# Building the rotation table in a later stage, spreading the head sums of the expert stage, and taking the layer norm's roots on GpSimd

## The chip, the cores and the metric

The kernel runs on one core of one Trainium2 chip. The metric is the device time of one execution in microseconds; three runs of the kernel before gave 1475.19, 1478.64 and 1481.58 us, so the median is 1478.64 us. The engines are named as in the profile: PE is TensorE's matmul, PEld its weight load, DVE is VectorE, ACT is ScalarE, POOL is GpSimd, and SP is the queue that issues the DMAs.

## The reference

The input is x, 1024 tokens of 512 features in fp32. Eight blocks follow each other, each as `x = layernorm(x + block(x))`, so nothing of one block can start on a tile before the norm of the block before it. What each computes:

- first block: two projections to 128 features, a series of powers of their difference, and a gated feed-forward with 1248 hidden features
- second block, the expert stage: a base product with `W_org`, plus eight low-rank experts whose weights come from a softmax of the mean token. One matrix is built, `w_eff = W_org + delta`, and each token tile is multiplied by it
- third block: attention over a sequence of length 1, so it is a product of x with values and output projection; for each of 8 key/value heads the 4 output matrices of its queries are added, and then merged with the value matrix
- fourth block: a feed-forward with 1792 hidden features whose weights are integers with a zero point and a scale for each group: `(w - z) * s`. This is the quantised feed-forward stage
- fifth block: a stack of four small layers with a long convolution. It needs a table of `p**n` for n from 0 to 1023 for 64 channels and 4 layers, with complex p. Its modulus is applied in a scan; its phase is the rotation table `wave`
- sixth block: a product with two low-rank parts; seventh: causal attention with 32 heads; eighth: a feed-forward with integer weights and one scale for each matrix

## The kernel before, in words

Each stage is a block of five instruction streams that meet at its end. x lies in two forms: `x_tok` (token tiles, 8 of 128x512) and `x_feat` (features on partitions, 128 x 4 x 1024). `x_feat` feeds the matmuls.

**Tail.** The end of every stage, for each token tile t: PE has written the product into one of two banks (`out_ready`); DVE adds it to `x_tok` (L92, or L95 and L97 with a bias), takes the statistics (L98, L99), waits for the standard deviation, takes its reciprocal (L101) and normalises (L102, `normed`). ACT takes the root (L108) and, for the tile before, copies the transposed tile from PSUM to `x_feat` (L115). PE transposes the normalised tile (L134). Each engine works through the tiles in order; DVE waits in place for the root.

**The expert stage** (`lora_then_single_key`). DVE reduces `x_feat` to its mean (L742), PE and DVE turn it into eight coefficients, DVE scales the experts' matrices `up` by them in eight instructions of 64 partitions (L759). Then DVE runs the first part of the rotation table (`Rotation.dve`, L913 to L946: 60 dependent instructions on 128x4 numbers, with two activations of ACT in between), while PE multiplies `down` with the scaled `up` (L694). DVE adds `W_org` (L766), and PE multiplies the eight token tiles by `w_eff` (L610). In the tail loop DVE does, after each tile, the sum of one head group for the next block: `lora_pair` (L774, 128x1024) and `lora_wo_sum` (L777, 128x512). Three buffers hold the heads' matrices, and SP waits for `paired` before it loads a fourth. GpSimd meanwhile doubles the table in ten levels (`Rotation.pool`, L970 to L976): six products on 4·2^level numbers in each level, three in the last, so up to 128x2048. After the tail PE merges the head sums with the value matrix (L707, 64 matmul records), DVE copies the result (L781) and a second tail follows with L610.

**The quantised feed-forward stage** (`swiglu` with `front1`, 14 tiles of hidden features). ACT rounds x to its high part (L379) and DVE subtracts for the low part (L475). For each hidden tile f DVE computes `w - z` (L440), times s (L443, and L445 for the down weights), ACT rounds (L388), DVE takes the low part (L457, `w_lo`). PE does gate and up for both halves of the tokens (48 matmuls, L346), ACT the silu (L395) into a single buffer `gate`, DVE the product with up (L464, `product`). The order on DVE and ACT is written out by hand:

```
split_w_up(0); low part of x; split_w_up(1); [extra_dve]
for each f: multiply(f) for both halves; split_w_up(f + 2)
```

PE may start tile f + 1 only when `product` of the first half of tile f is there, since it writes the same bank. z and s have one buffer each, and SP loads them for the next tile when L445 has used them. After the 14 tiles the hidden features are split into high and low parts (L286 on ACT, L289 on DVE), in two groups g for each token tile, PE multiplies them with the down weights (L363), and the tail runs beside it. PE's transpose of tile t - 1 stands between the two groups of tile t.

**Later stages.** The convolution stage starts when its own weights have landed; its DVE stream waits for the table (`half_ready`). Its tail, the tail of the sixth block and the last feed-forward use the same `Tail`. The causal attention takes its own roots on GpSimd, with an addition (L1507) and a power of -0.5 (L1510).

Of the kernel before, what the change touches and what calls it, by code (L numbers as in the profile page):

```python
# [14 lines left out]
F32 = mybir.dt.float32  # L15
# [19 lines left out]
class Chip:  # L35


    def __init__(self, nc, ctx):
# [13 lines left out]
        self.tails = self.ln_count = 0  # L52
# [10 lines left out]
class Tail:  # L63
# [6 lines left out]
    NAMES = ("out_ready", "out_taken", "ln_step", "var_ready", "std_ready", "normed", "transposed", "feat_ready")  # L70

    def __init__(self, chip, out_bank, tr_bank, last=False):
        self.c, self.out_bank, self.tr_bank, self.last = chip, out_bank, tr_bank, last

        (self.out_ready, self.out_taken, self.ln_step, self.var_ready, self.std_ready, self.normed,
         self.transposed, self.feat_ready) = chip.tail_sems
        self.base = NT * chip.tails
        chip.tails += 1

    def dve(self, dve, t, bias=None):  # L80
# [19 lines left out]
        dve.wait_ge(self.std_ready, self.base + t + 1)  # L100
        step(nc.vector.reciprocal(c.rstd[:, t:t + 1], c.std[:, t:t + 1]))  # L101
# [3 lines left out]
    def act_std(self, act, t):  # L105
# [3 lines left out]
                             bias=c.eps[:, 0:1]).then_inc(self.std_ready, 1)  # L109
# [7 lines left out]
    def act(self, act):  # L117
        for t in range(NT):
            self.act_std(act, t)
            if t and not self.last:  # L120
                self.act_copy(act, t - 1)
# [30 lines left out]
def setup(c):  # L152

    nc = c.nc
    c.eps = c.sb("eps", [P, 1], F32)
    ready, zeroed = c.sem("const_ready"), c.sem("ident_zeroed")
    with nc.Block() as block:

        @block.gpsimd
        def _(pool):  # L160
            nc.gpsimd.memset(c.eps[:, :], EPS)
            nc.gpsimd.memset(c.ident[:, :], 0.0).then_inc(zeroed, 1)
# [57 lines left out]
def swiglu(c, front, down=None, last=None, x_loaded=None, first_loads=None, extra_loads=None,  # L220
           extra_dve=None, extra_pe=None, extra_act=None):
# [15 lines left out]
    with ExitStack() as own:  # L237
# [24 lines left out]
        hidden = sb("hidden", [P, tiles, TOK], F32)  # L262
        g_bank, u_bank = c.bank[0:2], c.bank[2:4]
# [37 lines left out]
        with nc.Block() as block:  # L301

            @block.sync
            def _(sp):
# [18 lines left out]
                if last is not None:  # L323
# [3 lines left out]
                    sp.wait_ge(stored, 16 * NT)  # L327

# [45 lines left out]
            def _(act):  # L374
# [240 lines left out]
def lora_then_single_key(c, a, load_ahead):  # L615
# [16 lines left out]
    with ExitStack() as own:  # L632
# [12 lines left out]
        ones = sb("ones", [P, P])  # L645
# [9 lines left out]
        delta_ready, eff_ready, step = sem("delta"), sem("eff"), sem("step")  # L655

        with nc.Block() as block:

            @block.sync
            def _(sp):  # L660
# [4 lines left out]
                c.rot.load(sp, a)  # L665
                sp.dma_start(w_org[:, :, :], a["L0_org"]).then_inc(org_loaded, 16)
                sp.dma_start(wv[:, :, :], a["L1_wv"]).then_inc(wv_loaded, 16)
                for g in range(KV):
                    if g >= SLOTS:
                        sp.wait_ge(paired, g - SLOTS + 1)  # L670
                    sp.dma_start(wo[:, g % SLOTS, :, :], a["L1_wo"][g]).then_inc(wo_loaded[g % SLOTS], 16)
                load_ahead(sp)

            @block.gpsimd
            def _(pool):
                nc.gpsimd.memset(ones[:, :], 1.0).then_inc(ones_ready, 1)
                c.rot.pool(pool)

            @block.tensor
            def _(pe):  # L680
# [10 lines left out]
                pe.wait_ge(coeff_ready, 1)  # L691
# [40 lines left out]
            def _(dve):  # L732
# [9 lines left out]
                then(nc.vector.tensor_reduce(mean[:, :], c.x_feat[:, :, :], AX.X, ALU.add))  # L742
# [11 lines left out]
                then(nc.vector.tensor_scalar(coeff[:, :], e[:, :], inv[:, 0:1], None, ALU.mult))  # L754
                dve.wait_ge(w_loaded, 32)
                for r in range(RC):
                    for h in range(P // R):
                        rows, expert = slice(h * R, (h + 1) * R), r * (P // R) + h
                        ins = nc.vector.tensor_scalar(up_c[rows, r, :], up[rows, r, :],  # L759
                                                      coeff[rows, expert:expert + 1], None, ALU.mult)  # L760
                ins.then_inc(coeff_ready, 1)
                c.rot.dve(dve)
                dve.wait_ge(org_loaded, 16)
                for i in range(KC):
                    dve.wait_ge(delta_ready, i + 1)
                    nc.vector.tensor_tensor(w_eff[:, i, :], w_org[:, i, :], c.bank[i][:, :], ALU.add)\  # L766
                        .then_inc(eff_ready, 1)
                for t in range(NT):
                    tail.dve(dve, t)

                    dve.wait_ge(wo_loaded[t % SLOTS], 16 * (t // SLOTS + 1))
                    if t:
# [1137 lines left out]
```

## Time and profile before

| | us |
|---|---|
| median of three runs | 1478.64 |
| the profiled execution, whole time | 1483.27 |
| the profiled execution, span from first to last instruction | 1481.6 |
| first block | 0 to 250 |
| expert stage, with the merged attention | 250 to 402 |
| quantised feed-forward stage | 402 to 657 |
| convolution stage | 657 to 842 |
| sixth block | 842 to 890 |
| causal attention | 890 to 1283 |
| last feed-forward | 1283 to 1481 |

The profile is of one execution. Busy time is the time in which an engine had an instruction in work; for matmuls it is modelled, since they are pipelined. PEclk is the mean granted clock of TensorE as a share of full speed: its two levels are 1.2 and 2.4 GHz, so 0.75 of full speed in a window means that half of it ran at the lower level. A timeline row ends in brackets with the idle time before it and what ended it.

### The profile page before, as it was taken

The numbers are of one execution on the slowest core, as the hardware profiler recorded it, in microseconds if no ns is written. First come the engines' busy times: TensorE is split into PE (matmuls) and PEld (weight loads), VectorE is DVE, ScalarE is ACT, GpSimd is POOL, SyncE is SP. The second block draws the span as 40 slices with busy tenths as digits, with TensorE's granted clock in tenths as the row PEclk, the third lists the DMA queues.
The fourth block names the chain that finished last, engine by engine and source line by source line (L and its number), as shares of the span: only waits on it lengthen the run. The fifth ranks groups of instructions, "written<-read, shape, count | busy, mean of one in ns | idle before, by whom it ended". The sixth has DMA issues, their size and how long they took to land. (4 is left out here: it accounts for less than half of the span.)

```text
span 1481.6 us, 14589 instructions
## 1 busy us (share of the span) xinstructions
PE 1285.3 (87%) x5314; PEld 843.9 (57%) x5314; DVE 754.6 (51%) x1301; ACT 426.6 (29%) x709; POOL 142.2 (10%) x208
## 2 busy tenths in 40 slices
PE   7999997869799999973565698989999999699998
PEld 4787664324378887763443243444554553388877
DVE  5223323792655554423556563877777642433254
ACT  2122111100221214210221213136656666312141
POOL 0000000490000000001111004000101114000000
PEclk9999998889989999985566699989999999799999
DMA  7110002450066540004000001000000000021001
GB/s 304 43 42 0 0 0 71 196 195 0 5 222 220 208 153 0 1 15 141 1 0 0 0 0 43 1 1 2 1 2 2 3 3 1 24 83 64 21 19 38
DMA packets 18681, 78.82 MB, mean 53 GB/s; under 512 B 3330, under 2 KB 4226, under 8 KB 16452
## 3 DMA queue, kind: packets, MB, share of 16 engines
q1 hardware_dynamic: 18628, 78.13, 14.6%
q8 instruction: 32, 0.52, 0.1%
q14 instruction: 21, 0.17, 0.0%
HBM read 75.76 MB, written 2.10 MB: 53 GB/s over the span
## 5 line engine op out<-in xcount | busy, mean ns | idle before, releaser
L346 PE MATMUL psum<-L_ffn_x,L_ffn_w_up 128*128 128x512 f32 x1200 | 277.1, 394 | 16.2 <-DVE L_ffn_x L475 16.2
L346 PEld LDWEIGHTS psum<-L_ffn_x,L_ffn_w_up 128*128 128x128 f32 x1200 | 228.4, 191 | 64.5 <-issue 16.6
L1751 DVE TENSOR_REDUCE mqa_top<-psum 128x1 f32<-128x512 f32 (+3 forms) x304 | 186.0, 656 | 59.8 <-PE psum L1577 40.1
L1670 ACT ACTIVATE mqa_prob<-psum 128x512 f32<-128x512 f32 x288 | 160.1, 601 | 87.6 <-PE psum L1595 86.7
L363 PE MATMUL psum<-L_ffn_wd,L_ffn_part_h 128*128 128x512 f32 x600 | 141.6, 397 | 7.0 <-DVE L_ffn_wd L298 7.0
L1595 PE MATMUL psum<-mqa_stack,mqa_keys 100*128 100x512 f32 x288 | 132.7, 475 | 4.7 <-DMA mqa_stack<-mqa_rows 3.4
L363 PEld LDWEIGHTS psum<-L_ffn_wd,L_ffn_part_h 128*128 128x128 f32 x600 | 114.3, 192 | 31.6 <-DVE L_ffn_part_h L289 7.8
L1571 PE MATMUL psum<-mqa_keys,mqa_stack 96*128 96x512 f32 (+3 forms) x384 | 129.3, 384 | 2.3 <-DVE mqa_top L1751 1.0
L346 PE MATMUL psum<-L_attn_x,L_attn_w_up 128*128 128x512 f32 x480 | 111.3, 394 | 3.9 <-DVE L_attn_hidden L464 3.9
L346 PEld LDWEIGHTS psum<-L_attn_x,L_attn_w_up 128*128 128x128 f32 x480 | 91.2, 190 | 23.8 <-issue 4.8
L464 DVE TENSOR_TENSOR L_ffn_hidden<-L_ffn_gate,psum 128x512 f32 (+1 forms) x50 | 34.3, 686 | 138.3 <-PE psum L346 138.3
L1595 PEld LDWEIGHTS psum<-mqa_stack,mqa_keys 100*128 100x128 f32 x288 | 55.3, 196 | 72.0 <-ACT mqa_prob L1670 59.3
L1571 PEld LDWEIGHTS psum<-mqa_keys,mqa_stack 96*128 96x128 f32 x384 | 72.7, 196 | 25.4 <-DVE mqa_top L1751 14.6
L108 ACT ACTIVATE ln_std<-ln_mean_var,eps 128x1 f32<-128x1 f32 x56 | 16.5, 295 | 242.9 <-DVE ln_mean_var L99 242.9
L1608 PE MATMUL psum<-mqa_prob,mqa_v 128*32 128x512 f32 x576 | 77.7, 605 | 0.0
L1108 PE MATMUL psum<-ident,conv_twice 128*128 128x128 f32 x72 | 20.1, 434 | 54.7 <-DVE conv_twice L1220 54.7
L1503 POOL TENSOR_SCALAR_AFFINE_SELECT mqa_prob<-mqa_prob 128x512 f32<-128x512 f32 x64 | 39.8, 640 | 269.6 <-ACT mqa_prob L1670 269.5
L134 PE MATMUL psum<-ident,x_tok 128*128 128x128 f32 x192 | 33.6, 302 | 36.4 <-DVE x_tok L102 35.9
L289 DVE TENSOR_TENSOR L_ffn_part_h<-L_ffn_hidden,L_ffn_part_h 128x896 fp32r<-128x896 f32 (+2 forms) x32 | 31.7, 991 | 58.0 <-ACT L_ffn_part_h L286 58.0
L363 PE MATMUL psum<-L_attn_wd,L_attn_part_h 128*128 128x512 f32 x240 | 61.1, 407 | 0.0
L388 ACT CAST L_ffn_w_up<-L_ffn_stage 128x1024 fp32r<-128x1024 f32 x25 | 26.3, 1050 | 121.0 <-DVE L_ffn_stage L443 81.8
L134 PEld LDWEIGHTS psum<-ident,x_tok 128*128 128x128 f32 x192 | 24.0, 152 | 63.0 <-DVE x_tok L102 57.5
(237 smaller groups left out, 1611.0 us busy)
## 6 DMA issues: line engine op xcount, KB each, us to landing
L_ffn_stage<-in_L_w SPq DMA_DIRECT2D x25, 768.0 KB, 6.6
L_ffn_z_int<-in_L_z SPq DMA_DIRECT2D x14, 768.0 KB, 4.4
L_ffn_s_all<-in_L_s SPq DMA_DIRECT2D x14, 768.0 KB, 6.1
lora_wo<-in_L_wo SPq DMA_DIRECT2D x8, 1024.0 KB, 4.9
L_attn_stage<-in_L_w SPq DMA_DIRECT2D x10, 512.0 KB, 3.6
L_attn_w_down<-in_L_down SPq DMA_DIRECT2D x1, 2560.0 KB, 24.8
x_feat<-in_x_feat SPq DMA_DIRECT2D x2, 1024.0 KB, 7.1
x_tok<-in_x_tok SPq DMA_DIRECT2D x1, 2048.0 KB, 19.2
```

The costliest lines, as they stand in the source:

```text
L134: ins = nc.tensor.transpose(self.tr_bank[t % 2][:, k * P:(k + 1) * P], c.x_tok[:, t, k * P:(k + 1) * P], c.ident[:, :])
L289: nc.vector.tensor_tensor(part_h[:, g, 1, 0:n, :], src, part_h[:, g, 0, 0:n, :].bitcast(F32), ALU.subtract).then_inc(h_lo, 1)
L346: ins = nc.tensor.matmul(bank[half][:, :], w_up[:, slot, w_part, at:at + P], x[:, x_part, k, half * HALF:(half + 1) * HALF], start=k == 0 ...
L363: ins = nc.tensor.matmul(tail.out_bank[t % 2][:, :], part_h[:, g, h_part, f - groups[g].start, :], wd[:, w_part, f, :], start=f == 0 and n ...
L388: nc.scalar.copy(w_up[:, slot, 0, :], stage[:, slot, 0:up_width]).then_inc(w_hi, 1)
L464: nc.vector.tensor_tensor(hidden[:, f, half * HALF:(half + 1) * HALF], gate[:, :], u_bank[half][:, :], ALU.mult).then_inc(product, 1)
L1503: nc.gpsimd.affine_select(out=tile, in_=tile, compare_op=ALU.is_ge, fill=0.0, base=0, pattern=[[0, 4], [1, P]], channel_multiplier=-1).the ...
L1571: ins = nc.tensor.matmul(out[:, at * width:(at + 1) * width], stack[0:SPLIT, head // 2, cols(qt)], keys[0:SPLIT, head % 2, lo:lo + width], ...
L1595: ins = nc.tensor.matmul(score_bank[n % 3], keys[0:SHIFTED, head, cols(kt)], stack[0:SHIFTED, 4 * g:4 * g + 4, cols(qt)], start=True, stop ...
L1608: nc.tensor.matmul(value_bank[row:row + 32, :], v[:, kt, :], prob[:, n % PROBS, :], start=kt == 0, stop=final).then_inc(value_done, 1)
L1670: nc.scalar.activation(prob[:, n % PROBS, :], score_bank[n % 3], ACT.Exp, scale=SCALE)\
L1751: nc.vector.tensor_reduce(top[:, i % 2, lo // HALF, heads[0]:heads[-1] + 1], max_bank[n % 3][:, 0:len(heads) * width] .rearrange("p (h k) ...
```

## The change

- `Rotation` is no longer built in the expert stage. The quantised feed-forward stage gets it through its hooks: the load of its parameters behind the loads for hidden tile 1, `Rotation.dve` on DVE after `split_w_up(1)`, `Rotation.act` on ACT in the same place, `Rotation.pool` on GpSimd once both halves of x are split. Its two big scratch arrays are no longer arrays of their own but views of `x_feat`, which nobody reads from then to the tail. ACT waits for the table's end (`feat_free`) before it splits the hidden features.
- In the expert stage the mean is reduced half by DVE, half by ACT (a copy with an accumulated sum); the scaled `up` is made half by DVE, half by ACT; the head sums are done one before the first `w_eff` tile, one after each of its first two, one after token tiles 2, 4, 6 and 7, and one after the tail. The loads of the heads come earlier in SP's order, those of `W_org` and the value matrix later.
- In every `Tail` the root is no longer ACT's square root and DVE's reciprocal but two GpSimd instructions: the addition of eps, and the power of -0.5. DVE still waits for it in place.

The diff, cut to its core:

```diff
@@ class Tail
-        dve.wait_ge(self.std_ready, self.base + t + 1)
-        step(nc.vector.reciprocal(c.rstd[:, t:t + 1], c.std[:, t:t + 1]))
+        dve.wait_ge(self.rstd_ready, self.base + t + 1)
+        if self.root_on_act:
+            step(nc.vector.reciprocal(c.rstd[:, t:t + 1], c.std[:, t:t + 1]))
         nc.vector.tensor_scalar(row, row, c.mean_var[:, t, 0:1], c.rstd[:, t:t + 1],
                                 ALU.subtract, ALU.mult).then_inc(self.normed, 1)
+    def pool(self, pool):
+        c, nc = self.c, self.c.nc
+        for t in range(NT):
+            pool.wait_ge(self.var_ready, self.base + t + 1)
+            nc.gpsimd.tensor_tensor(c.std[:, t:t + 1], c.mean_var[:, t, 1:2], c.eps[:, 0:1], ALU.add)\
+                .then_inc(self.var_eps, 1)
+            c.var_eps += 1
+            pool.wait_ge(self.var_eps, c.var_eps)
+            nc.gpsimd.tensor_tensor(c.rstd[:, t:t + 1], c.std[:, t:t + 1], c.half_power[:, :], ALU.pow)\
+                .then_inc(self.rstd_ready, 1)
@@ def swiglu
+            @block.gpsimd
+            def _(pool):
+                if extra_pool is not None:
+                    pool.wait_ge(x_lo, base["x_lo"] + 2)
+                    extra_pool(pool)
+                tail.pool(pool)
@@ act, before the split of the hidden features
+                if feat_free is not None:
+                    act.wait_ge(feat_free, 1)
@@ act, in the token loop
-                    tail.act_std(act, t)
@@ def lora_then_single_key, sync
-                c.rot.load(sp, a)
-                sp.dma_start(w_org[:, :, :], a["L0_org"]).then_inc(org_loaded, 16)
-                sp.dma_start(wv[:, :, :], a["L1_wv"]).then_inc(wv_loaded, 16)
                 for g in range(KV):
                     if g >= SLOTS:
                         sp.wait_ge(paired, g - SLOTS + 1)
                     sp.dma_start(wo[:, g % SLOTS, :, :], a["L1_wo"][g]).then_inc(wo_loaded[g % SLOTS], 16)
+                    if g == 1:
+                        sp.dma_start(w_org[:, :, :], a["L0_org"]).then_inc(org_loaded, 16)
+                    if g == SLOTS:
+                        sp.dma_start(wv[:, :, :], a["L1_wv"]).then_inc(wv_loaded, 16)
@@ gpsimd
-                c.rot.pool(pool)
+                tail.pool(pool)
+                tail_values.pool(pool)
@@ scalar
+                for k in range(2, KC):
+                    nc.scalar.activation(wide_sum[:, k - 2, :], c.x_feat[:, k, :], ACT.Copy,
+                                         accum_out=mean[:, k:k + 1]).then_inc(mean_by_act, 1)
...
-                c.rot.act(act)
+                act.wait_ge(w_loaded, 32)
+                act.wait_ge(step, COEFF_STEP)
+                for r in range(RC):
+                    ins = nc.scalar.activation(up_c[0:R, r, :], up[0:R, r, :], ACT.Copy,
+                                               scale=coeff[0:R, 2 * r:2 * r + 1])
+                ins.then_inc(coeff_ready, 1)
@@ vector
-                then(nc.vector.tensor_reduce(mean[:, :], c.x_feat[:, :, :], AX.X, ALU.add))
+                then(nc.vector.tensor_reduce(mean[:, 0:2], c.x_feat[:, 0:2, :], AX.X, ALU.add))
+                dve.wait_ge(mean_by_act, 2)
...
-                c.rot.dve(dve)
+                add_heads(0)
                 dve.wait_ge(org_loaded, 16)
                 for i in range(KC):
                     dve.wait_ge(delta_ready, i + 1)
                     nc.vector.tensor_tensor(w_eff[:, i, :], w_org[:, i, :], c.bank[i][:, :], ALU.add)\
                         .then_inc(eff_ready, 1)
+                    if i in (0, 1):
+                        add_heads(i + 1)
                 for t in range(NT):
                     tail.dve(dve, t)
+                    if t in (2, 4, 6, 7):
+                        add_heads(3 + (2, 4, 6, 7).index(t))
+                add_heads(7)
@@ class Rotation, scratch
-        self.other = c.sb("rot_other", [P, C_DEPTH, TOK // 2], F32, own)
-        self.tmp = c.sb("rot_tmp", [P, C_DEPTH, TOK // 2], F32, own)
+        self.other, self.tmp = (c.x_feat[:, 2 * i:2 * i + 2, :].rearrange("p a (b n) -> p (a b) n", b=2)
+                                for i in range(2))
@@ def build
-            lora_then_single_key(c, a, front1.load_first)
-        swiglu(c, front1)
+        lora_then_single_key(c, a, front1.load_first)
+        swiglu(c, front1, extra_scratch=c.rot.scratch, extra_loads=lambda sp: c.rot.load(sp, a),
+               extra_dve=c.rot.dve, extra_act=c.rot.act, extra_pool=c.rot.pool, feat_free=c.rot.half_ready)
```

`add_heads(g)` is the pair of DVE instructions of L774 and L777 with their waits.

## Rows read from the trace of the kernel before

**Rows 1.** Busy time by window: PE, PEld, DVE, ACT, POOL; then PEclk, DMA share, GB/s.

```profile
250.00:402.00 152.00, 119.50 (x298) 55.25 (x298) 95.47 (x181) 18.29 (x39) 53.30 (x68) 0.87 0.29 113
402.00:655.00 253.00, 238.14 (x1036) 194.47 (x1036) 132.31 (x156) 64.49 (x91) 0.00 (x0) 0.97 0.33 118
```

**Rows 2.** Timeline, expert stage up to its first products: start, duration, instruction, idle before.

```profile
250.18 4.42 DVE L742 TENSOR_REDUCE lora_mean<-x_feat 128x4 f32<-128x4096 f32 x1 [1.91 <-PEq L301]
...
259.47 3.96 DVE L759 TENSOR_SCALAR lora_up_c<-lora_up,lora_coeff 64x512 f32<-64x512 f32 x8 [0.16 <-DMA lora_down<-in_L_lora_down]
263.58 16.77 PE L694 MATMUL psum<-lora_up_c,lora_down 128*128 128x512 f32 x32 [5.62 <-DVE lora_up_c L759]
...
281.13 7.13 PE L610 MATMUL psum<-lora_w_eff,x_feat 128*128 128x512 f32 x16 [0.78 <-DVE lora_w_eff L766]
```

**Rows 3.** Timeline, expert stage, DVE and POOL together, and PE's merge.

```profile
325.96 4.58 POOL L972 TENSOR_TENSOR wave<-wave,rot_tmp 128x2048 f32<-128x2048 f32 x1
326.08 5.54 DVE L774 TENSOR_TENSOR lora_pair<-lora_wo 128x1024 f32<-128x1024 f32 x1
334.91 1.22 DVE L774 TENSOR_TENSOR lora_pair<-lora_wo 128x1024 f32<-128x1024 f32 x1
335.96 9.49 PE L707 MATMUL psum<-lora_wo_sum,lora_wv 128*128 128x512 f32 x16
345.72 20.77 PE L707 MATMUL psum<-lora_wo_sum,lora_wv 128*128 128x512 f32 x48
```

**Rows 4.** Timeline, second tail of that stage, one of its tiles on DVE.

```profile
382.20 0.69 DVE L92 TENSOR_TENSOR x_tok<-x_tok,psum 128x512 f32<-128x512 f32 x1 [1.13 <-PE psum L610]
```

**Rows 5.** Timeline, first and last of the 60 DVE instructions of the rotation.

```profile
263.46 0.16 DVE L913 SCALAR_TENSOR_TENSOR rot_small<-rot_par 128x4 f32<-128x4 f32 x1
...
275.21 0.17 DVE L946 COPY rot_small<-rot_small 128x4 f32<-128x4 f32 x1
```

**Rows 6.** Timeline, DVE in the quantised feed-forward stage.

```profile
412.51 1.76 DVE L440 TENSOR_TENSOR L_ffn_stage<-L_ffn_stage,L_ffn_z_int 128x1536 f32<-128x1536 int32 x1 [0.44 <-DMA L_ffn_s_all<-in_L_s]
...
416.64 1.23 DVE L457 TENSOR_TENSOR L_ffn_w_up<-L_ffn_stage,L_ffn_w_up 128x1024 fp32r<-128x1024 f32 x1 [0.51 <-ACT L_ffn_w_up L388]
...
424.07 0.69 DVE L464 TENSOR_TENSOR L_ffn_hidden<-L_ffn_gate,psum 128x512 f32<-128x512 f32 x1 [4.75 <-PE psum L346]
```

**Rows 7.** Busy time by window of PE alone, from its first matmul of that stage: PE, PEclk, DMA.

```profile
409.90:424.00 14.10, 13.99 (x49) 0.78 0.70 265
424.00:435.00 11.00, 11.00 (x50) 1.00 0.52 174
```

**Rows 8.** POOL's groups by form: busy us, mean ns, idle before.

```profile
L971 POOL TENSOR_TENSOR wave<-wave,rot_turn 128x2048 f32<-128x2048 f32 x1 | 3.9, 3929 | 0.1
L970 POOL TENSOR_TENSOR rot_tmp<-rot_other,rot_turn 128x1024 f32<-128x1024 f32 x1 | 1.9, 1892 | 0.1
```

**Rows 9.** Timeline, DVE's wait for the root: by ACT, then by POOL in attention.

```profile
399.69 0.16 DVE L101 RECIPROCAL ln_rstd<-ln_std 128x1 f32<-128x1 f32 x1 [0.36 <-ACT ln_std L108]
399.88 0.55 DVE L102 TENSOR_SCALAR x_tok<-x_tok,ln_mean_var,ln_rstd 128x512 f32<-128x512 f32 x1
...
1280.84 0.55 DVE L1792 TENSOR_SCALAR x_tok<-x_tok,ln_mean_var,ln_rstd 128x512 f32<-128x512 f32 x1 [0.93 <-POOL ln_rstd L1510]
```

**Rows 10.** Timeline, tail of the quantised feed-forward stage: one turn of its loop.

```profile
600.97 0.94 ACT L286 CAST L_ffn_part_h<-L_ffn_hidden 128x896 fp32r<-128x896 f32 x1 [4.06 <-PE psum L363]
...
605.14 0.55 DVE L102 TENSOR_SCALAR x_tok<-x_tok,ln_mean_var,ln_rstd 128x512 f32<-128x512 f32 x1
...
605.75 0.42 PEld L134 LDWEIGHTS psum<-ident,x_tok 128*128 128x128 f32 x4 [0.47 <-DVE x_tok L102]
```

**Rows 11.** Timeline, the additions of two tiles in the convolution's tail.

```profile
829.20 0.68 DVE L92 TENSOR_TENSOR x_tok<-x_tok,psum 128x512 f32<-128x512 f32 x1
...
831.85 0.68 DVE L92 TENSOR_TENSOR x_tok<-x_tok,psum 128x512 f32<-128x512 f32 x1
```

**Rows 12.** Timeline, the addition of one tile in the sixth block's tail.

```profile
869.11 0.69 DVE L95 TENSOR_TENSOR x_tok<-x_tok,psum 128x512 f32<-128x512 f32 x1 [0.41 <-PE psum L610]
```

**Rows 13.** The page, part 6, DMA issues of the expert stage: KB each, us from issue to landing.

```profile
lora_wo<-in_L_wo SPq DMA_DIRECT2D x8, 1024.0 KB, 4.9
```

More of the change, by code:

```diff
@@ L51, in __init__ @@
         self.ffn_base["loaded"] = [0, 0]
-        self.tails = self.ln_count = 0
+        self.tails = self.ln_count = self.var_eps = 0
         psum = ctx.enter_context(nc.psum_tensor("psum", [P, 8, 512], F32))
@@ L63, with __init__ @@
 class Tail:
-    NAMES = ("out_ready", "out_taken", "ln_step", "var_ready", "std_ready", "normed", "transposed", "feat_ready")
-    def __init__(self, chip, out_bank, tr_bank, last=False):
+    NAMES = ("out_ready", "out_taken", "ln_step", "var_ready", "var_eps", "rstd_ready", "normed", "transposed",
+             "feat_ready")
+    def __init__(self, chip, out_bank, tr_bank, last=False, root_on_act=False):
         self.c, self.out_bank, self.tr_bank, self.last = chip, out_bank, tr_bank, last
-        (self.out_ready, self.out_taken, self.ln_step, self.var_ready, self.std_ready, self.normed,
+        self.root_on_act = root_on_act
+        (self.out_ready, self.out_taken, self.ln_step, self.var_ready, self.var_eps, self.rstd_ready, self.normed,
          self.transposed, self.feat_ready) = chip.tail_sems
@@ L220, in swiglu @@
 def swiglu(c, front, down=None, last=None, x_loaded=None, first_loads=None, extra_loads=None,
-           extra_dve=None, extra_pe=None, extra_act=None):
+           extra_dve=None, extra_pe=None, extra_act=None, extra_pool=None, extra_scratch=None,
+           feat_free=None):
     nc = c.nc
@@ L262, in swiglu @@
         hidden = sb("hidden", [P, tiles, TOK], F32)
+        if extra_scratch is not None:
+            extra_scratch(own)
         g_bank, u_bank = c.bank[0:2], c.bank[2:4]
@@ L754, in _, with add_heads @@
                 then(nc.vector.tensor_scalar(coeff[:, :], e[:, :], inv[:, 0:1], None, ALU.mult))
+                assert count == COEFF_STEP, count
                 dve.wait_ge(w_loaded, 32)
                 for r in range(RC):
[L757 to L760, printed above, removed]
+                    ins = nc.vector.tensor_scalar(up_c[R:P, r, :], up[R:P, r, :], coeff[R:P, 2 * r + 1:2 * r + 2],
+                                                  None, ALU.mult)
                 ins.then_inc(coeff_ready, 1)
-                c.rot.dve(dve)
+                def add_heads(g):
+                    dve.wait_ge(wo_loaded[g % SLOTS], 16 * (g // SLOTS + 1))
+                    if g:
+                        dve.wait_ge(summed, g)
+                    nc.vector.tensor_tensor(pair[:, :, :], wo[:, g % SLOTS, 0:2, :], wo[:, g % SLOTS, 2:4, :],
+                                            ALU.add).then_inc(paired, 1)
+                    dve.wait_ge(paired, g + 1)
+                    nc.vector.tensor_tensor(wo_sum[:, g, :], pair[:, 0, :], pair[:, 1, :], ALU.add)\
+                        .then_inc(summed, 1)
+                add_heads(0)
                 dve.wait_ge(org_loaded, 16)
@@ L767, in _ @@
                         .then_inc(eff_ready, 1)
+                    if i in (0, 1):
+                        add_heads(i + 1)
                 for t in range(NT):
                     tail.dve(dve, t)
-                    dve.wait_ge(wo_loaded[t % SLOTS], 16 * (t // SLOTS + 1))
-                    if t:
-                        dve.wait_ge(summed, t)
-                    nc.vector.tensor_tensor(pair[:, :, :], wo[:, t % SLOTS, 0:2, :], wo[:, t % SLOTS, 2:4, :],
-                                            ALU.add).then_inc(paired, 1)
-                    dve.wait_ge(paired, t + 1)
-                    nc.vector.tensor_tensor(wo_sum[:, t, :], pair[:, 0, :], pair[:, 1, :], ALU.add)\
-                        .then_inc(summed, 1)
+                    if t in (2, 4, 6, 7):
+                        add_heads(3 + (2, 4, 6, 7).index(t))
+                add_heads(7)
                 for i in range(KC):
@@ L820, in two_loras, with _ @@
         with nc.Block() as block:
+            @block.gpsimd
+            def _(pool):
+                tail.pool(pool)
             @block.tensor
@@ L1089, in _ @@
                 root(2 * C_DEPTH)
+                tail.pool(pool)
             @block.tensor
```

21 lines of the change are left out of this document (10 added, 11 removed).

## The prediction

> **What bounds the kernel now.** I read the windows by stage first. PE is busy 119.5 of the expert stage's 152 us, and 238.1 of 253 us in the quantised feed-forward stage, whose clock is 0.97; the reader is to see that only the first has much to give, and that DVE (95 us) and POOL (53 us) work beside each other there [rows 1]. The timeline of the expert stage says why PE waits. An instruction of L774 takes 1.22 us alone, and 5.54 us while POOL's L972 runs (325.96 to 330.54); it ends 1.1 us after POOL does [rows 3]. So the two do not share, one waits for the whole instruction of the other, and between two of POOL's a DVE instruction gets its turn. L92, which reads PSUM, keeps its 0.68 us throughout. From the first product's end at about 284.9 (281.13 plus half of 7.13 [rows 2]) to the start of the merge at 335.96 [rows 3] eight tiles take 51 us, 6.4 each, while in the second tail a tile is 3.87: 2.74 of DVE and 1.13 of waiting for PE, which is the bound there [rows 4].
>
> In the quantised stage PE runs without a gap, 48 matmuls in 10.9 us, once started [rows 7]. DVE is busy 7.4 of each 10.9: it is off the path by 3.5 us a tile. The table goes there.
>
> **The change, part by part.** Times are those of the profiled execution (1483.27, span 1481.6).
>
> *The front of the expert stage: -1.6.* Half the mean on ACT saves half of 4.42, but DVE already waits 0.16 for `lora_down` before L759 [rows 2]; that load keeps its place in SP's order, so only 0.16 is saved there. Of the eight L759 instructions (3.96) DVE keeps four, 2.0; ACT's four are not in the trace. ACT's L286 takes 0.94 for 896 columns [rows 10], so 0.6 for 512, and I take 2.4; bounds 2.0 to 4.0. -1.6 at PE's start; the 16.77 of L694 only moves. L913 to L946 took DVE from 263.46 to 275.4 [rows 5], wholly beside L694, whose last tile decides (280.4): removing it saves nothing. The first three head sums (1.22 + 0.69 each) go into that same cover. `W_org` now lands behind two head loads of 1 MB; a head load takes 4.9 from issue to landing [rows 13], in a queue of several at once, so an estimate of 10 us for both puts it before 268, and up to about 275 nothing waits, since only the last of the four additions decides.
>
> *The tails of the expert stage: -23.2.* Without POOL a DVE tile is 2.65 (L92 to L92, [rows 11]), plus 0.37 for the new root (below), so 3.0. Head sums of 1.9 after tiles 2, 4 and 6 make two tiles 7.9 against PE's 7.7; two product banks cover the difference. So 3.9 a tile. First output at 284.9 - 1.6 = 283.3; seven more are out at 310.7, the transposes of tile 6 make it 311.1. Before 335.96, less 1.6: 24.8 - 1.6 = 23.2. The heads' loads (SP waits for `paired`) are each asked 8 us or more ahead. The sums behind tile 7 end at 318.6, PE wants the last at about 335.
>
> *The merge: -2.6.* The first 16 records took 9.49, where 48 took 20.77, so 6.9 for 16 [rows 3]: PE had waited for L102 before and came at a low clock. That wait is gone. The second tail stays PE-bound (3.0 against 3.87). Expert stage: **-27.4**; bounds -20 (tiles at 4.5, clock not gained) to -30.
>
> *`Rotation.dve` in the quantised stage: +9.4.* DVE ends `split_w_up(1)` at 417.87 and has 60 instructions before it, 11.9 us: until 429.7, then L464 until 430.4. Before, PE ended tile 0 at 424.0 and went on at once, since that product had been made early [rows 6]. It now waits 6.4 us. ACT's roots and three table loads end by 423 and hide under this. After 8.9 us of idling PE's first tile took 14.0 instead of 10.9 with a granted clock of 0.78 [rows 7]: +3.1; before L694 it had idled 5.6 and lost 2.9. I take +3.0 for 6.4. Bounds 6.4 to 9.5.
>
> *`Rotation.pool` beside DVE: +12.5.* Each hidden tile has four DVE instructions with two SBUF inputs (L440 1.76, L443 1.2, L445 0.7, L457 1.23 [rows 6]), like L774. Each can wait for one whole instruction of POOL, and then POOL takes the port before the next. Levels 0 to 6 are POOL instructions of 0.2 to 0.6 us: up to 2.4 a tile, inside the 3.5. They last until about 456. Level 7, six of some 1.05: 4.2 in the tile, covered by 3.5 and the early finish before it. Level 8, six of 1.89, and level 9, three of about 3.65 alone (3.9 with waits) [rows 8]: one tile meets four of 1.9, 7.6 us, less 3.5 and about 0.3 of lag: 3.8 late. The next meets two of 1.9 and two of 3.65, 11.1, less 3.5, less 2.0 by which the low clock stretches PE's tile, less 0.9 for the one already under way: 4.7 late. The ninth-level instruction that is left falls in a tile with cover. Two waits of 4 us: two low-clock starts. The merge above lost 2.6 after 3 us; I take 2.0 each. 8.5 + 4.0 = 12.5. Bounds: 0, and, if all fifteen of levels 7 to 9 (28.6 us) are met, less 3.5 in four tiles, 14.6 plus three starts of 3.0, 23.6. Table complete at about 500, `feat_free` asked at 566: free.
>
> L440 reads int32, and no row shows such a one beside POOL. The Trainium skill (SBUF — State Buffer, "SBUF: two separate sides") calls the pair of ports between the two engines "an exclusive lock, not a bandwidth split", taken by any DVE instruction with two SBUF inputs. By that rule L440 counts and the sum stays; if it did not, each tile would meet three: 5.7 less 3.5 less 0.3 is 1.9, the next 9.2 less 3.5 less 0.9 is 4.8, and with one low-clock start the sum would have 8 to 9 in place of 12.5. The trace agrees for fp32 (5.54 against 1.22).
>
> *The roots: +7.8.* DVE waits 0.36 for ACT and then spends 0.16 + 0.04 on L101: 0.56. Where POOL makes the root, it waits 0.93 [rows 9]: **+0.37** a tile. Bounds: 0.2, 0.6. Where does it show? In the quantised stage's tail a turn is a closed chain: output, ACT L286 at 600.97, DVE L289, L92 to L102 (ends 605.69), PEld L134 at 605.75 having waited 0.47 for it [rows 10], then PE's second group, next output. Seven turns and the end: 8 x 0.37 = 3.0. The convolution's tail is DVE's alone, 2.65 a tile [rows 11]: 8 x 0.37 = 3.0. In the sixth block DVE waits only 0.41 a tile [rows 12]: 0.37 nearly fills that, and I take 0.7 with its end. First block, second tail of the expert stage and the last feed-forward: only the last tile, 1.1. ACT's five table loads for the root all lay in idle time and give nothing.
>
> **Sum:** -27.4 + 9.4 + 12.5 + 7.8 = **+2.3**, so 1485.6 for an execution like the profiled one. That one was 4.6 over the median of 1478.64; on the median it is **1481.0**.
>
> **The rivals.**
> - *The lock does not reach PE.* For: DVE has 3.5 us spare a tile, two buffers of `w_up`, and many of POOL's instructions fall in DVE's free time. Against: four instructions a tile, and POOL lost no turn in [rows 3]. Then 12.5 falls to 0 to 3: 1481.0 - 11 = 1470 (faster).
> - *The lock and the clock take more* (slower). POOL's three long instructions all meet one hidden tile: 3 x 3.65 + 1.9 = 12.9, less 3.5: 9.4; the tile before 7.9 - 3.5 = 4.4; starts 3 + 2. That is 18.8 in place of 12.5, and 1487.3. It decides once the first level-9 instruction is asked within the four of one tile, which a shift of 1 to 2 us in POOL's start brings about. With five percent longer POOL instructions too, 1491.
> - *The expert stage gives less.* DVE stays the bound of its tails at 4.5 a tile (8 x 0.6 = 5) because the loads of heads wait on `paired`, and the merge keeps its low clock (2.6): 1488.6. Against: all these loads have slack above.
> - *Nothing of it does what it says*, the table still waits in the expert stage: no, the queues show its instructions gone.
>
> **How the numbers follow.** 0.5% is 7.4 us, about what can be told from no change. Forecast, 0.45: 1481, own range 1474 to 1486. Lock not felt, 0.25: 1467 to 1474. Lock and clock, 0.18: 1486 to 1494. Less from the expert stage, 0.12: 1484 to 1493. The unknown sizes (12.5 between 0 and 23.6, 27.4 between 20 and 30) would allow 1466 to 1500; their far ends together are unlikely: range **1466 to 1494**. Faster than 1471.2: 0.22. Slower than 1486.0: 0.30. Between: 0.48.
>
> **What would show it.** Expert stage about 125 us instead of 152, L774 at 1.22 throughout, L707 in one run of 28. In the quantised stage a PE gap of 6 us before its second hidden tile; L440 to L457 of 2 to 5 us around the fifth and sixth, gaps of 4 there, none later. DVE idle 0.93 before each L102, the turn of that stage's tail 10.6 instead of 10.25, the convolution's tail 3.0 a tile. Wrong if L440 keeps 1.76 beside a long POOL instruction, if PE's gap before tile 1 is absent, or if the expert tails stay over 4.5.

## The result, and the profile after

The changed kernel takes **1481.99 us** (median of 20 runs, 1478.29 to 1486.42); the kernel before, beside it, 1478.39 (20 runs). The ratio is 1.0027, 95% interval [1.0017, 1.0036]: 4 us slower, inside the 0.5% that the prediction called the same. Forecast: 1481.0, as +2.3 on 1478.64. The profiled execution took 1483.97 (span 1482.2, clock 0.906), against 1483.27 (1481.6) before.

Busy time by window of the kernel after (columns as in [rows 1]). The first window starts as there and ends 27 us earlier; the second is as long as there:

```profile
250.00:375.00 125.00, 109.83 (x298) 51.92 (x298) 59.17 (x101) 15.25 (x26) 12.02 (x33) 0.92 0.34 137
375.38:628.00 252.62, 223.28 (x942) 181.38 (x943) 150.29 (x193) 59.60 (x81) 66.81 (x77) 0.93 0.33 119
```

The expert stage has lost its POOL work (53.30 to 12.02) and 27 us. The quantised stage has it now (0 to 66.81), PE is busy 223.28 instead of 238.14 of as many microseconds, and its clock fell from 0.97 to 0.93: a window of that length no longer holds the whole stage.

The path of PE through the expert stage (timeline: start, duration, instruction, idle before), to be laid beside [rows 2, 3]:

```profile
262.70 16.39 PE L724 MATMUL psum<-lora_up_c,lora_down 128*128 128x512 f32 x32 [6.64 <-ACT lora_up_c L763]
...
279.87 7.13 PE L637 MATMUL psum<-lora_w_eff,x_feat 128*128 128x512 f32 x16 [0.78 <-DVE lora_w_eff L816]
...
311.22 7.03 PE L737 MATMUL psum<-lora_wo_sum,lora_wv 128*128 128x512 f32 x16
```

The product with `w_eff` (L637) starts 1.3 earlier than before, the merge (L737) 24.7 earlier, and its first 16 records take 7.03, not 9.49. On DVE, in the same stretch, a tile with a head sum and one without:

```profile
293.94 1.22 DVE L806 TENSOR_TENSOR lora_pair<-lora_wo 128x1024 f32<-128x1024 f32 x1
...
295.80 0.68 DVE L94 TENSOR_TENSOR x_tok<-x_tok,psum 128x512 f32<-128x512 f32 x1
...
298.36 0.55 DVE L105 TENSOR_SCALAR x_tok<-x_tok,ln_mean_var,ln_rstd 128x512 f32<-128x512 f32 x1 [0.93 <-POOL ln_rstd L122]
298.82 0.68 DVE L94 TENSOR_TENSOR x_tok<-x_tok,psum 128x512 f32<-128x512 f32 x1
...
303.70 0.68 DVE L94 TENSOR_TENSOR x_tok<-x_tok,psum 128x512 f32<-128x512 f32 x1
```

From addition to addition (L94) it is 3.02 us without a head sum and 4.88 with one. The sum's first instruction (L806) takes its 1.22, and DVE waits 0.93 for the root.

PE in the quantised stage, every run of matmuls that began after an idle time until the end of the up phase:

```profile
383.65 12.73 PE L372 MATMUL psum<-L_ffn_x,L_ffn_w_up 128*128 128x512 f32 x48 [8.87 <-DVE L_ffn_x L502]
404.17 45.35 PE L372 MATMUL psum<-L_ffn_x,L_ffn_w_up 128*128 128x512 f32 x192 [7.79 <-DVE L_ffn_hidden L491]
452.79 13.96 PE L372 MATMUL psum<-L_ffn_x,L_ffn_w_up 128*128 128x512 f32 x48 [3.27 <-DVE L_ffn_hidden L491]
470.97 89.57 PE L372 MATMUL psum<-L_ffn_x,L_ffn_w_up 128*128 128x512 f32 x384 [4.22 <-DVE L_ffn_hidden L491]
```

The 7.79 stands behind the 60 instructions of `Rotation.dve`, which begin and end so on DVE:

```profile
391.50 0.15 DVE L963 SCALAR_TENSOR_TENSOR rot_small<-rot_par 128x4 f32<-128x4 f32 x1
...
403.26 0.17 DVE L996 COPY rot_small<-rot_small 128x4 f32<-128x4 f32 x1
403.34 0.69 DVE L491 TENSOR_TENSOR L_ffn_hidden<-L_ffn_gate,psum 128x512 f32<-128x512 f32 x1
```

The lock is the name used here for what [rows 3] showed: of a DVE and a POOL instruction that meet, one waits for the other. It stands behind the 3.27 and the 4.22. DVE before the first of them:

```profile
441.76 1.90 DVE L467 TENSOR_TENSOR L_ffn_stage<-L_ffn_stage,L_ffn_z_int 128x1536 f32<-128x1536 int32 x1 [2.21 <-DMA L_ffn_s_all<-in_L_s]
...
443.69 3.31 DVE L470 TENSOR_TENSOR L_ffn_stage<-L_ffn_stage,L_ffn_s_all 128x1024 f32<-128x1024 f32 x1
...
446.93 2.38 DVE L472 TENSOR_TENSOR L_ffn_w_down<-L_ffn_stage,L_ffn_s_all 128x512 f32 x1
...
449.23 2.91 DVE L484 TENSOR_TENSOR L_ffn_w_up<-L_ffn_stage,L_ffn_w_up 128x1024 fp32r<-128x1024 f32 x1
```

DVE and POOL before the second:

```profile
454.44 3.60 POOL L1020 TENSOR_TENSOR x_feat<-x_feat,rot_turn 128x2048 f32<-128x2048 f32 x1
456.21 3.45 DVE L467 TENSOR_TENSOR L_ffn_stage<-L_ffn_stage,L_ffn_z_int 128x1536 f32<-128x1536 int32 x1 [1.95 <-DMA L_ffn_s_all<-in_L_s]
458.12 5.00 POOL L1021 TENSOR_TENSOR wave<-wave,rot_turn 128x2048 f32<-128x2048 f32 x1
459.69 4.51 DVE L470 TENSOR_TENSOR L_ffn_stage<-L_ffn_stage,L_ffn_s_all 128x1024 f32<-128x1024 f32 x1
463.20 5.44 POOL L1022 TENSOR_TENSOR wave<-wave,x_feat 128x2048 f32<-128x2048 f32 x1
464.12 5.07 DVE L472 TENSOR_TENSOR L_ffn_w_down<-L_ffn_stage,L_ffn_s_all 128x512 f32 x1
469.11 1.21 DVE L484 TENSOR_TENSOR L_ffn_w_up<-L_ffn_stage,L_ffn_w_up 128x1024 fp32r<-128x1024 f32 x1
```

Read the ends: L470 ends 1.08 after POOL's L1021 (464.20, 463.12), L472 0.55 after L1022. Each ended within its own time (1.23, 0.68) of the other's end. POOL's instructions waited in turn: L1021 took 5.00 and stood for 1.54 of it beside L467 (which ended at 459.66), L1022 5.44, of which 1.00 beside L470.

Not all of DVE's lateness is waiting for POOL. In both tiles L467 first waited for the load of the scales, 2.21 and 1.95 us. z and s have one buffer, so that load is asked only when L472 of the tile before has ended (449.31; asked at 449.46 and 449.89, there at 456.2). A late L472 makes the next tile's load late as well.

### The profile page after: what moved, and what is told of

Same layout as the page of the kernel before. It is cut to its first block and busy times, and to the rows that moved or that the text cites. A ratio compares the mean times of both kernels' runs of the same rounds, so it can differ in the third digit from the quotient of the medians.

```text
span 1482.2 us, 14587 instructions
## 1 busy us (share of the span) xinstructions
PE 1286.5 (87%) x5314; PEld 844.7 (57%) x5314; DVE 740.3 (50%) x1241; ACT 406.7 (27%) x652; POOL 193.5 (13%) x320
## 5 line engine op out<-in xcount | busy, mean ns | idle before, releaser
L372 PE MATMUL psum<-L_ffn_x,L_ffn_w_up 128*128 128x512 f32 x1200 | 283.3, 399 | 31.5 <-DVE L_ffn_x L502 16.2
L372 PEld LDWEIGHTS psum<-L_ffn_x,L_ffn_w_up 128*128 128x128 f32 x1200 | 232.1, 194 | 82.5 <-issue 25.0
L118 POOL TENSOR_TENSOR ln_std<-ln_mean_var,eps 128x1 f32<-128x1 f32 x56 | 10.6, 190 | 779.5 <-DVE ln_mean_var L101 779.5
L129 ACT COPY x_feat<-psum 128x512 f32<-128x512 f32 x48 | 28.0, 584 | 200.5 <-PE psum L149 200.5
L421 ACT ACTIVATE L_ffn_gate<-psum 128x512 f32<-128x512 f32 x50 | 29.8, 596 | 107.6 <-PE psum L372 87.5
```

Source lines behind the costliest of these rows:

```text
L129: nc.scalar.copy(c.x_feat[:, :, t * P:(t + 1) * P], src).then_inc(self.feat_ready, 1)
L372: ins = nc.tensor.matmul(bank[half][:, :], w_up[:, slot, w_part, at:at + P], x[:, x_part, k, half * HALF:(half + 1) * HALF], start=k == 0 ...
L421: nc.scalar.activation(gate[:, :], g_bank[half][:, :], ACT.Silu).then_inc(gated, 1)
```

## The experiments

The ratio is always to the kernel before, on the same chip; "against the changed kernel" is the difference of two such ratios times 1478 us, good to about 3 us.

**Roots on ScalarE again.** ACT makes the root and DVE its reciprocal, in every tail but attention's, the quantised one's included; POOL's part of `Tail` goes.

```
-    def __init__(self, chip, out_bank, tr_bank, last=False, root_on_act=False):
+    def __init__(self, chip, out_bank, tr_bank, last=False, root_on_act=True):
...
                     if t + 1 < NT:
                         split_h(act, t + 1, 1, 0)
+                    if tail.root_on_act:
+                        tail.act_std(act, t)
```

> The changed kernel (1482.0) with one part undone: all tails take the root by ACT's square root and DVE's reciprocal again. Theory: the root on GpSimd costs 0.37 us wherever DVE's chain is closed; against the trace of before, the changed kernel lost 3.1 in the tail of the quantised stage, 2.6 in the convolution's, 1.3 in the sixth block's and 0.4 at each of three other ends. So 1482.0 - 8 = 1474 (1473 to 1476), ratio to before 0.997. Rival: DVE is not the bound of most tails, the wait is hidden, and the trace's shifts are chance: 1480 to 1482.

Measured: 1471.34 us, ratio 0.9958 [0.9943, 0.9974], 10 us less than the changed kernel. In the convolution's tail (timeline, DVE; first the kernel after, then this one):

```profile
819.64 0.68 DVE L94 TENSOR_TENSOR x_tok<-x_tok,psum 128x512 f32<-128x512 f32 x1
...
822.20 0.55 DVE L105 TENSOR_SCALAR x_tok<-x_tok,ln_mean_var,ln_rstd 128x512 f32<-128x512 f32 x1 [0.94 <-POOL ln_rstd L122]
822.66 0.68 DVE L94 TENSOR_TENSOR x_tok<-x_tok,psum 128x512 f32<-128x512 f32 x1
```

```profile
819.26 0.16 DVE L104 RECIPROCAL ln_rstd<-ln_std 128x1 f32<-128x1 f32 x1 [0.36 <-ACT ln_std L111]
819.46 0.55 DVE L105 TENSOR_SCALAR x_tok<-x_tok,ln_mean_var,ln_rstd 128x512 f32<-128x512 f32 x1
```

0.94 of waiting against 0.36 + 0.16 + 0.04: the 0.37 a tile of the prediction. Stretch by stretch, the changed kernel's trace is longer than this one by 0.4 in the first block, 0.7 and 0.8 in the two tails of the expert stage, 3.3 in the quantised tail, 2.2 in the convolution's, 1.1 in the sixth block's and 0.4 at the end: 8.8 us. That the roots cost about what they were said to is shown; 10 with an error of 3 holds the 7.8 forecast.

**The table in pieces.** Each multiplication of `Rotation.pool` is cut into pieces of 64 columns (256 elements a partition); nothing else.

```
+PIECE = 64
...
-            src, dst = slice(0, n), slice(n, 2 * n)
-            then(mul(tmp[:, :, src], other[:, :, src], sin, ALU.mult))
+            for at in range(0, n, PIECE):
+                src, dst = slice(at, min(n, at + PIECE)), slice(n + at, n + min(n, at + PIECE))
+                then(mul(tmp[:, :, src], other[:, :, src], sin, ALU.mult))
...
```

> The changed kernel (1482.0) with the GpSimd instructions of the three largest doubling levels cut into pieces of 256 numbers (60 pieces of about 0.6 us instead of 15 of 1.0 to 3.6); the same work and a little more GpSimd time. Theory (a DVE instruction waits for one whole GpSimd instruction): each of four DVE instructions a hidden tile waits at most 0.7, 2.8 a tile, under DVE's 3.5 us of spare time, so both gaps of PE around tiles 5 and 6 (3.3 and 4.2) and the two low-clock starts (5.6) go: 1482.0 - 13 = 1469 (1467 to 1472). Rival (the two engines share a bandwidth, so what counts is the total GpSimd work in the stage): 1482 to 1486, the gaps smaller but more.

Measured: 1468.89 us, ratio 0.9957 [0.9940, 0.9974]. PE's second run of matmuls now has no end before the phase has:

```profile
403.91 143.19 PE L372 MATMUL psum<-L_ffn_x,L_ffn_w_up 128*128 128x512 f32 x624 [7.89 <-DVE L_ffn_hidden L491]
```

In the changed kernel the same 624 matmuls lie between 404.17 and 560.54, 156.4 us: 13.2 more, of which 7.5 are gaps and 5.7 low clock. DVE's groups around levels 8 and 9 (busy us, mean ns), of the kernel after (440 to 500 us) and of this one (420 to 500):

```profile
L470 DVE TENSOR_TENSOR L_ffn_stage<-L_ffn_stage,L_ffn_s_all 128x1024 f32<-128x1024 f32 x5 | 11.5, 2298 | 0.2
...
L472 DVE TENSOR_TENSOR L_ffn_w_down<-L_ffn_stage,L_ffn_s_all 128x512 f32 x5 | 9.5, 1900 | 0.0
```

```profile
L470 DVE TENSOR_TENSOR L_ffn_stage<-L_ffn_stage,L_ffn_s_all 128x1024 f32<-128x1024 f32 x8 | 11.8, 1481 | 0.3
...
L472 DVE TENSOR_TENSOR L_ffn_w_down<-L_ffn_stage,L_ffn_s_all 128x512 f32 x7 | 7.6, 1093 | 0.0
```

POOL has as much to compute and is busy longer (69.95 us of the window 375 to 480 instead of 63.09, and 21.36 instead of 5.19 of the next 170). It is not POOL's time in all that cost PE anything, but the length of a single instruction of POOL against the time that DVE has to spare in a tile.

**The table without its long levels.** Levels 7 to 9 are left out, so that the scan starts from an incomplete table (the array is filled with ones early on).

```
-        for level in range(self.LEVELS):
+        for level in range(7):
```

> The changed kernel (1482.0) without the three largest doubling levels on GpSimd (the rest of the rotation table is only filled with ones, in the expert stage, so the result is another). Theory: PE's gaps around hidden tiles 5 and 6 and their low clock come from these levels alone: 1482.0 - 13 = 1469, as with the pieces. Rival: the gaps come from the z and s loads that wait for L472 (DVE waited 2.2, 2.0 and 3.6 us for them): 1476 to 1480, and the gaps stay in part.

Measured: 1469.79 us, ratio 0.9948 [0.9930, 0.9967].

```profile
402.26 144.60 PE L372 MATMUL psum<-L_ffn_x,L_ffn_w_up 128*128 128x512 f32 x624 [8.07 <-DVE L_ffn_hidden L491]
```

That gap is the last one of the up phase here too, though levels 0 to 6 still meet DVE. Leaving the long levels out gives what cutting them gives, within the error. The whole of that term came from them. The recorded rival, that the loads of z and s make the gaps, fails as far as the loads alone go: here L467 waits at most 0.57 for them, and in the run with pieces of 64 it waits up to 2.84 while PE runs without a gap. Their waits add to a tile that the lock has made late; no run gave z and s a second buffer, so the size of that part is not tested.

**Pieces of 256 columns.** As above with `PIECE = 256`: level 9's three instructions are halved, to the length of level 8's; level 8 is untouched.

> Changed kernel with pieces of 256 columns (1024 elements a partition), so that only the three instructions of level 9 are cut, in two; level 8 keeps its length. Theory (the price goes by the longest POOL instruction that the four DVE instructions of one tile meet, and PE has 3.5 us of cover): level 9's waits halve and their gap of 4.2 us goes with its low clock, level 8's gap of 3.3 us with its low clock stays: -6, 1476, ratio 0.9985. Rival (any shortening is enough, or it is POOL's total that counts): as pieces of 64, ratio 0.996, or nothing at all, 1.003.

Measured: 1478.24 us, ratio 1.0005 [0.9992, 1.0017], 3 less than the changed kernel.

```profile
454.20 12.56 PE L372 MATMUL psum<-L_ffn_x,L_ffn_w_up 128*128 128x512 f32 x48 [3.06 <-DVE L_ffn_hidden L491]
468.49 87.33 PE L372 MATMUL psum<-L_ffn_x,L_ffn_w_up 128*128 128x512 f32 x384 [1.73 <-DVE L_ffn_hidden L491]
```

Level 8's gap stays (3.06), level 9's falls from 4.22 to 1.73. I expected it to go and a gain of 6: instructions of 1.89 still make a tile late behind one that has used the spare time up, and L467 again waited for the scales (1.85 us at 457.51). The order 64, 256, uncut (ratios 0.9957, 1.0005, 1.0027) fits the length of the longest instruction.

**`Rotation.dve` back in the expert stage.** Its first twelve instructions before L797, the other 48 behind it and beside PE's L724; the load, the small tensors and ACT's two steps go with it. POOL's part stays.

```
                 assert count == COEFF_STEP, count
+                turning = c.rot.dve(dve)
+                next(turning)
                 dve.wait_ge(w_loaded, 32)
...
-                add_heads(0)
+                next(turning, None)
                 dve.wait_ge(org_loaded, 16)
...
-                    if i in (0, 1):
-                        add_heads(i + 1)
+                    if i < KC - 1:
+                        add_heads(i)
```

> The changed kernel (1482.0) with the rotation's DVE and ACT parts back in the expert stage (the first 12 DVE instructions where DVE waits for lora_down, the other 48 beside L724, one head sum after each of the first three w_eff tiles); only the GpSimd part stays in the quantised stage. Theory: the gap of PE before hidden tile 1 (6.5) and its low clock (1.9) go, and nothing comes in the expert stage, since its DVE is idle there: 1482.0 - 8.4 = 1473.6 (1472 to 1476). Rival: the expert stage gets longer by what the 60 instructions push back (w_eff, head sums, the loads that wait for them): 1478 to 1484.

Measured: 1473.38 us, ratio 0.9966 [0.9949, 0.9982], 9 less than the changed kernel.

```profile
384.92 45.70 PE L372 MATMUL psum<-L_ffn_x,L_ffn_w_up 128*128 128x512 f32 x192 [8.87 <-DVE L_ffn_x L502]
433.03 12.77 PE L372 MATMUL psum<-L_ffn_x,L_ffn_w_up 128*128 128x512 f32 x48 [2.41 <-DVE L_ffn_hidden L491]
450.26 99.84 PE L372 MATMUL psum<-L_ffn_x,L_ffn_w_up 128*128 128x512 f32 x432 [4.46 <-DVE L_ffn_hidden L491]
```

PE goes through four tiles in one run: the 7.79 before tile 1 is gone. The stage starts 1.3 us later (384.92 for 383.65), but this start scatters: the two runs in pieces, whose kernels are the changed one up to there, have it at 383.39 and 385.07. POOL starts earlier by what `Rotation.dve` was moved up, its long levels meet other tiles, and the two gaps stay, 6.9 us instead of 7.5. So the sixty small instructions cost about 9 us more in the one place than in the other, and what they cost in the expert stage is too small to be told from the scatter.

**All three cures.** Roots on ScalarE, `Rotation.dve` in the expert stage and pieces of 64, by the edits above.

> Changed kernel with the three cures of the first experiments together: roots on ScalarE, Rotation.dve back in the expert stage, the table's multiplications in pieces of 64 columns (256 elements a partition). Theory (the three prices stand in different places and add up; each cure alone gave a ratio of about 0.993 to the changed kernel): quantised stage without a gap of PE anywhere (7.8 + 7.5 us of gaps and some 6 us of low clock gone), +1.3 in the expert stage, roots -8: 1452 to 1456, ratio to the kernel before 0.983. Rival (one cure eats what another gave: with Rotation.dve gone POOL starts 12 us earlier and meets other tiles, and a PE without pauses is granted less clock later): 1461 or more, ratio 0.989.

Measured: **1454.85 us** (4 runs, 1451.03 to 1455.67), ratio 0.9848 [0.9832, 0.9865]: faster than both kernels. All 672 matmuls of the up phase are one run:

```profile
383.36 155.46 PE L372 MATMUL psum<-L_ffn_x,L_ffn_w_up 128*128 128x512 f32 x672 [8.87 <-DVE L_ffn_x L504]
```

The three cures alone gave 10.2, 10.3 and 9.0 against the changed kernel, 29.5; together 26.5. They add up within the error. No gap of PE was traded for another.

**The kernel before, in pieces.** The same cut of the table's multiplications in the kernel before, where they run beside the expert stage's tails.

> Kernel before, with nothing changed but the table's multiplications in pieces of 64 columns, still beside the expert stage's tails. Theory (a DVE instruction waits for one whole POOL instruction, so the length of that one is the price): L774 falls from a mean of 2.6 us to about 1.7 and L777 from 1.87 to about 1.1, some 2 us a tile, eight tiles: -12 to -16, about 1463, ratio 0.990. Rival (in a stage that DVE bounds, the two only take turns, and what counts is POOL's time in all, which pieces make longer): -3 or less, 1474, ratio 0.998 or more.

Measured: 1463.71 us, ratio 0.9911 [0.9895, 0.9927]. DVE's groups in those tails, of the kernel before (262 to 336 us), then of this one (262 to 350):

```profile
L774 DVE TENSOR_TENSOR lora_pair<-lora_wo 128x1024 f32<-128x1024 f32 x7 | 18.3, 2619 | 0.0
L777 DVE TENSOR_TENSOR lora_wo_sum<-lora_pair 128x512 f32<-128x512 f32 x6 | 11.2, 1866 | 0.2
L102 DVE TENSOR_SCALAR x_tok<-x_tok,ln_mean_var,ln_rstd 128x512 f32<-128x512 f32 x7 | 7.3, 1041 | 0.3
```

```profile
L774 DVE TENSOR_TENSOR lora_pair<-lora_wo 128x1024 f32<-128x1024 f32 x8 | 12.8, 1603 | 0.0
L777 DVE TENSOR_TENSOR lora_wo_sum<-lora_pair 128x512 f32<-128x512 f32 x8 | 8.5, 1065 | 0.3
```

And PE's merge, 15.4 earlier than in [rows 3] (1.0 of it was there before the tails, at L610: 280.16 for 281.13), its first 16 records at the full clock:

```profile
320.54 7.03 PE L707 MATMUL psum<-lora_wo_sum,lora_wv 128*128 128x512 f32 x16
```

The rival (what counts is POOL's time in all) falls: POOL works longer, and the kernel is 13 us faster. Cutting fifteen instructions in the kernel before was worth more than the whole change, which cost 4.

**A head sum after each tile.** The changed kernel with its eight sums where they were.

```
-                add_heads(0)
...
-                    if i in (0, 1):
-                        add_heads(i + 1)
...
-                    if t in (2, 4, 6, 7):
-                        add_heads(3 + (2, 4, 6, 7).index(t))
-                add_heads(7)
+                    add_heads(t)
```

> Changed kernel, but each token tile of the expert stage's first tail is followed by one head sum again, as before. Theory (a tile of that tail is the larger of DVE's 3.0 + 1.9 with a sum and PE's 3.9, so the spreading is worth 1 us a tile): merge about 6 us later, 1488, ratio 1.007. Rival (DVE catches up in PE's waits and the whole gain of that stage came from the table's leaving it): no change against the changed kernel, ratio 1.003.

Measured: 1486.69 us, ratio 1.0064 [1.0048, 1.0079], 5.5 more than the changed kernel. PE's turns in the tail, and its merge:

```profile
297.62 0.66 PE L149 MATMUL psum<-ident,x_tok 128*128 128x128 f32 x4 [0.79 <-DVE x_tok L105]
...
302.50 0.66 PE L149 MATMUL psum<-ident,x_tok 128*128 128x128 f32 x4 [0.79 <-DVE x_tok L105]
...
317.63 7.03 PE L737 MATMUL psum<-lora_wo_sum,lora_wv 128*128 128x512 f32 x16
```

A turn is 4.88 (3.0 and 1.9), and the merge is 6.4 later (311.22), 1.1 of which the start of L637 already had (280.94 for 279.87). From L637 to the merge it is 36.7 us here, 31.4 in the changed kernel and 54.8 before. So of the 23.5 us that the tails gained, the spreading made some 5, the table's absence 18.

## Why the prediction was right, step by step

| step | predicted | measured |
|---|---|---|
| front of the expert stage | -1.6 | -1.3 (L724 0.9 and L637 1.26 earlier), within the scatter |
| its first tail | -23.2 | -23.5 (merge 24.74 earlier, less 1.26) |
| merge | -2.6 | -2.5 (9.49 became 7.03) |
| second tail | 0 | +0.8 (quantised stage 26.4 earlier, not 27.2) |
| `Rotation.dve` | +6.4 gap, +3.0 clock | +6.5, +1.9 |
| `Rotation.pool` | +8.5 gaps, +4.0 clock | +7.5, +5.6 |
| roots: quantised tail | +3.0 | +3.15 |
| roots: convolution | +3.0 | +2.6 |
| roots: sixth block | +0.7 | +1.3, and 0.4 of clock |
| sum | +2.3 | +2.6 at the end of the sixth block |

The measured column is the shift of a landmark of one profiled execution against that of the other. Attention and the last block then gave 2.0 back in these two executions, 1.4 of it in a last down phase of 60.4 instead of 61.8 us; the medians differ by 3.6. How far one execution can be trusted shows at L637, which the kernels in pieces, unchanged up to there, start at 280.06 and 281.35, and the kernel before in pieces at 280.16: the gain of the front is not shown.

*The mechanism.* The forecast rested on one reading of [rows 3]: one engine waits until the instruction of the other has ended. Cutting the instructions showed it in both stages, with all the same work done. The rival "the lock does not reach PE" (1470) failed: the waits of two tiles were longer than DVE's spare time. The condition of "the lock and the clock take more" (1487 to 1491) did come true: all three of POOL's longest instructions met one tile, where the forecast had two. Its price did not: they cost 9.4 us of waits, not 12.9, since L467 was asked 1.8 us after POOL's instruction had begun and waited for the rest alone, and L484 found POOL done (1.21). "The expert stage gives less" failed at turns of 3.0 and 4.9.

*Where the sum was lucky.* The gaps of `Rotation.pool` came out at 7.5 for 8.5 by terms that were off and cancelled. The prediction gave DVE 3.5 us to spare in a tile, as busy 7.4 of 10.9. Its own four durations and two products of 0.69 add up to 6.3, DVE is busy 6.05 of the 11 us from 424 to 435, and this is what it had left in the kernel before:

```profile
434.95 0.69 DVE L464 TENSOR_TENSOR L_ffn_hidden<-L_ffn_gate,psum 128x512 f32<-128x512 f32 x1 [4.32 <-PE psum L346]
```

So 4.3, not 3.5. The first late tile was to lose 7.6 us by the lock; it lost 5.6 (0.14, 2.08, 1.70 and 1.68 over the four instructions' own times) and 2.2 by the load of the scales, which the prediction put at nothing. The second was to lose 11.1; it lost 9.4 and 1.95. 7.8 less 4.3 is 3.5 for a gap of 3.27; 11.3 less 4.3, less 3.2 by which PE's own tile was longer (13.96 for 10.75), is 3.8 for a gap of 4.22. The mechanism held, and that its price was met so closely is luck.

*The int32 instruction.* L467 took 3.45 us beside POOL and 1.76 without it, and ended 1.6 after POOL's L1020 (459.66, 458.04): it waited. By the rule of the Trainium skill weighed in the prediction (SBUF — State Buffer, "SBUF: two separate sides") it counts among the four; the trace agrees.

*What was mis-sized.* The clock. 3.0 was taken for the start behind `Rotation.dve` from the start in [rows 7], 2.0 for each of the later two from the merge, which had lost 2.6 after 3 us of waiting. Three windows of the kernel after, the first tile behind the 7.79, the tile behind that, and the tile behind the 3.27 (all engines, then PEclk):

```profile
404.17:417.05 12.88, 12.88 (x50) 10.54 (x51) 6.16 (x7) 2.69 (x4) 10.61 (x30) 0.87 0.53 185
417.05:427.80 10.75, 10.75 (x49) 8.91 (x48) 6.46 (x6) 2.14 (x3) 9.89 (x12) 1.00 0.46 148
452.79:466.75 13.96, 13.96 (x48) 10.94 (x48) 11.20 (x4) 2.14 (x3) 13.72 (x4) 0.79 0.31 118
```

Against the 10.75 of a tile at full clock the long gap cost 2.1 us, the short one 3.2. The two errors cancelled in the sum (7.0 forecast, 7.5 measured).

Not settled: the roots cost 7 us in the three tails of the table, 8.8 over all stretches against the run without them, and 10 in the medians, whose error is 3; and why cutting to 64 gained 13.6 us in its trace by the end of the stage and 10 in the medians. Both may be that error alone.

## What to carry to other kernels

Before a block of GpSimd work is moved out of the way of VectorE, cut its instructions. At each meeting the lock costs at most the rest of one instruction of the other engine, so the price goes with the length of the longest ones and not with their sum. When the waits of a tile stay below the time that VectorE has to spare in it (4.3 us here), they cost nothing. Look also at what a late instruction holds up: here a load with one buffer added about 2 us to each late tile. Small instructions in number (sixty at 0.2 us) belong where the engine waits for another anyway; their place was worth 9 us here. A step that repeats in every tail is priced by the kinds of loop it stands in: 0.37 us a tile showed in full where the tail was a closed chain or DVE's alone, and for two or three tiles elsewhere.

## What the runs showed of the hardware

- The lock stretches both sides. POOL's L1021 took 5.00, where the same multiplication took 3.93 in the kernel before [rows 8]; DVE's L472 took 5.07 against 0.68. With pieces of 64 L472 still has a mean of 1.09.
- An instruction pays for what is left of the other's. L467 was asked 1.77 after L1020 (3.60) had begun, and waited 1.69.
- A TENSOR_SCALAR with one tensor in SBUF and two scalars for each partition waited too. From the kernel before:

```profile
303.36 1.89 POOL L970 TENSOR_TENSOR rot_tmp<-rot_other,rot_turn 128x1024 f32<-128x1024 f32 x1
...
304.25 1.28 DVE L102 TENSOR_SCALAR x_tok<-x_tok,ln_mean_var,ln_rstd 128x512 f32<-128x512 f32 x1
```

It takes 0.55 alone [rows 9] and ended here 0.28 after POOL did; its mean in those tails was 1.04, while BATCH_NORM_STATS2 over the same row kept its 0.69 (one kernel; no run tried it apart). The prediction had not counted it; the quantised stage's up phase has none.
- What TensorE's low clock costs after an idle time is not told by that time's length: 12.88 us for a tile behind 7.8 us, 13.96 behind 3.3, and 12.73 behind 8.87, where the kernel before took 14.0 behind the same 8.87 and the last experiment 13.84.
